# Joining pairs of states on VectorE before the accumulating transfer, in a Mamba and mixture-of-experts block

## The reference

```python
h = layernorm(x) * (1 + ca) + sa
x = x + ga * attn(h)                      # a Mamba layer
h = layernorm(x) * (1 + cb) + sb
x = x + gb * ffn(h)                       # a mixture of experts

# attn: 512 inner channels, 16 states
xi, z = split(rmsnorm(h) @ in_proj.T)
xi = silu(causal_conv4(xi))
dt, Bm, Cm = split(xi @ x_proj.T)         # 16, 16, 16
delta = softplus(dt @ dt_proj.T + b)
for every token:                          # per channel d and state s
    s = s * exp(delta * A) + delta * Bm * u
    y = sum_s(s * Cm)
y = (y + u * D) * silu(z);  out = y @ out_proj.T + h

# ffn: 16 experts, 4 of them per token, and a shared one of 256
g = sigmoid(h @ gate_w.T);  top4 of g, normalized -> combine
routed = sum_e combine_e * (silu(h @ win_e) * (h @ vin_e)) @ wout_e
```

## Time and profile before

| | |
|---|---|
| time, median of 3 runs | 2876.76 us (2871.17 to 2878.23) |
| the profiled execution | 2876.35 us, its span 2874.6 us |
| busy over the span | PE 2407.7 us, POOL 2400.2, DVE 2274.8, ACT 2127.2 |
| instructions | 52662 |
| mean granted TensorE clock | 0.943 of full speed |
| DMA | 456.03 MB, 159 GB/s |

### The profile page before, as it was taken

One profiled execution on the slowest core, in us unless ns is written; L12 is line 12 of the kernel. 1 busy time (PEld: TensorE's weight loads), 2 busy tenths in 40 slices (PEclk: granted clock), 3 DMA queues, 4 the chain that ended last, 5 costly groups with the idle time before them and its releaser, 6 DMA issues.

```text
span 2874.6 us, 52662 instructions
## 1 busy us (share of the span) xinstructions
PE 2407.7 (84%) x16372; PEld 1915.6 (67%) x16372; DVE 2274.8 (79%) x3495; ACT 2127.2 (74%) x4033; POOL 2400.2 (83%) x2382
## 2 busy tenths in 40 slices
PE   4557989879798897979889798988979888797989
PEld 1335767768576775857667576766857677585868
DVE  5777878788787878778787887878878787887853
ACT  4787877778687777877778787777868777786641
POOL 1887998889888898988989899898979988897942
PEclk7668999999999999999999999999999999999999
DMA  2786767867676785777768676786767777676841
GB/s 74 197 178 141 172 154 170 185 140 171 147 171 160 174 184 132 173 169 161 165 150 189 145 172 158 168 185 136 180 147 170 162 171 180 137 171 154 192 101 60
DMA packets 154565, 456.03 MB, mean 159 GB/s; under 512 B 22280, under 2 KB 24968, under 8 KB 154032
## 3 DMA queue, kind: packets, MB, share of 16 engines
q0 software_dynamic: 73728, 268.47, 49.1%
q1 hardware_dynamic: 80560, 184.20, 20.5%
HBM read 166.29 MB, written 17.87 MB: 64 GB/s over the span
## 4 chain that ended last, share of the span: by engine, by line
POOL 49%; issue 29%; DMA 10%; PE 2%; ACT 2%; DVE 2%; POOLq 1%; DVEq 0%; ACTq 0%; SPq 0%
POOL db_sb L701 26%; DMA y_sb<-c_rows 9%; POOL y_sb L713 9%; POOL act L744 7%; POOL y_sb L722 2%; POOL du_sb L688 2%; DMA w_sb<-w_dram 1%; POOL conv L679 1%; PE bank_ps L1461 1%; DVE states L1186 1%; POOLq L698 1%; PE moe_ps L1479 1%; POOL rstd L729 1%; PE bank_ps L1414 0%; ACT da_ps L945 0%
## 5 line engine op out<-in xcount | busy, mean ns | idle before, releaser
L701 POOL TENSOR_TENSOR db_sb<-du_sb,b_sb 128x512 f32<-128x512 f32 x1024 | 1653.2, 1991 | 103.8 <-DVE states L1186 103.2
L713 POOL DMA_DIRECT2D y_sb<-c_rows x512 | 745.1, 1455 | 159.7 <-DMA y_sb<-c_rows 92.9
L918 ACT ACTIVATE c_rows<-rows_ps,xd_sb 128x512 f32<-128x512 f32 x1024 | 687.0, 684 | 169.3 <-DMA y_sb<-c_rows 100.6
L744 POOL TENSOR_TENSOR act<-act,w_sb 128x256 f32<-128x256 f32 x512 | 689.3, 1515 | 119.6 <-DVE act L1273 97.2
L945 ACT ACTIVATE da_ps<-delta,a_sb 128x512 f32<-128x512 f32 x1024 | 702.9, 690 | 64.4 <-DVE states L1186 60.4
L1387 PE MATMUL rows_ps<-ident,states 128*128 128x128 f32 x4096 | 614.5, 287 | 145.2 <-DVE states L1186 91.4
L1461 PE MATMUL bank_ps<-h2T_high,ein_w_high 128*128 128x256 f16 x2304 | 638.2, 277 | 57.9 <-DVE act L1273 31.1
L1186 DVE TENSOR_TENSOR_SCAN states<-da_ps,carry,db_sb 128x512 f32<-128x512 f32 x512 | 643.9, 1274 | 26.1 <-ACT da_ps L945 18.5
L1479 PE MATMUL moe_ps<-eout_sb,act 128*128 128x256 f32 x2304 | 589.8, 388 | 75.0 <-POOL act L744 52.9
L1387 PEld LDWEIGHTS rows_ps<-ident,states 128*128 128x128 f32 x4096 | 502.1, 148 | 225.2 <-DVE states L1186 97.8
L1186 DVE TENSOR_TENSOR_SCAN states<-da_ps,db_sb 128x512 f32<-128x512 f32 x512 | 612.4, 1213 | 41.1 <-ACT da_ps L945 33.4
(11 more groups left out here) (170 smaller groups left out, 2678.5 us busy)
## 6 DMA issues: line engine op xcount, KB each, us to landing
y_sb<-c_rows POOLq DMA_DIRECT2D x512, 512.0 KB, 6.3
b_sb<-b_dram SPq DMA_DIRECT2D x128, 512.0 KB, 5.5
w_sb<-w_dram SPq DMA_DIRECT2D x256, 256.0 KB, 4.0
th_p<-x_dram SPq DMA_DIRECT2D x16, 512.0 KB, 6.9
r_dram<-conv SPq DMA_DIRECT2D x16, 512.0 KB, 2.9
x<-r_dram SPq DMA_DIRECT2D x16, 512.0 KB, 4.6
out_dram<-x SPq DMA_DIRECT2D x32, 256.0 KB, 4.7
mod_p<-mod_dram SPq DMA_DIRECT2D x7, 384.0 KB, 8.9
```

Of the source, the lines that this page charges most:

```text
L701: pool.tensor_tensor(db_sb[:, n % NDB, :], du_sb[:, slots[t][0][0], b, :], b_sb[:, k % NBPAIR, s % BPAIR, :], ALU.mult).then_inc(sem["scal ...
L713: pool.dma_start(y_sb[:, slots[t][0][0], CPAIR * pair:CPAIR * pair + CPAIR, :], c_rows[:, n % NCR, :, :], accum_op=ALU.add).then_inc(c_add ...
L744: pool.tensor_tensor(place, place, w_sb[:, k % NWROWS, n % WROWS, :], ALU.mult).then_inc(sem["e_weighed"], 1)
L918: ac.activation(c_rows[:, n % NCR, j % CPAIR, :], rows_ps[j % 2][:, :], ACT.Copy, scale=xd_sb[:, slots[t][0][0], j, s:s + 1]).then_inc(sem ...
```

## The change

Four things are changed.

1. For the states in `JOINED` (1, 5, 9, 13) the scaling by C_s is done on DVE instead of ACT, by an instruction that also adds the scaled rows of the state before, which lie in `c_rows`. The state before issues no transfer of its own; the transfer behind the joined state carries both.

```diff
+JOINED = (1, 5, 9, 13)
...
-            out.append((at + 0.145, ("c_scale", t, s, j)))
-            if j % CPAIR == CPAIR - 1:
+            out.append((at + 0.145, ("c_join" if s in JOINED else "c_scale", t, s, j)))
+            if j % CPAIR == CPAIR - 1 and s + 1 not in JOINED:
                 out.append((at + 0.892, ("c_add", t, s, j // CPAIR)))
...
             def c_scales(step, j):
-                return sem["c_scaled"], NJ * step + j + 1
+                k, s = divmod(step, NS)
+                joins = len(JOINED) * k + sum(q < s for q in JOINED)
+                if s in JOINED:
+                    return sem["c_joined"], NJ * joins + j + 1
+                return sem["c_scaled"], NJ * (step - joins) + j + 1
+
+            def piece(step, j):
+
+                k, s = divmod(step, NS)
+                return NJ // CPAIR * (step - len(JOINED) * k - sum(q <= s for q in JOINED)) + j // CPAIR
...
+                    def c_join(t, s, j):
+
+                        step = NS * nS(t) + s
+                        place = c_rows[:, piece(step, j) % NCR, j % CPAIR, :]
+                        v.wait_ge(sem["rows_full"], NJ * step + j + 1)
+                        v.wait_ge(*c_scales(step - 1, j))
+                        v.scalar_tensor_tensor(place, rows_ps[j % 2][:, :], xd_sb[:, slots[t][0][0], j, s:s + 1], place,
+                                               ALU.mult, ALU.add).then_inc(sem["c_joined"], 1)
```

```diff
-                        ac.activation(g_sb[:, :, :], bank(key)[:, 0:NJ * NE].rearrange("p (j e) -> p j e", j=NJ), ACT.Exp, scale=-1.0 / LIFT).then_inc(bank_read(key)[0], 1)
+                        ac.activation(bank(key)[:, 0:NJ * NE], bank(key)[:, 0:NJ * NE], ACT.Exp, scale=-1.0 / LIFT).then_inc(sem["logit_exped"], 1)
...
+                        exped, g, equal, rank = (bank(key)[:, n * NJ * NE:(n + 1) * NJ * NE] for n in range(4))
...
-                        done(v.tensor_scalar(g_sb[:, :, :], g_sb[:, :, :], 1.0, None, ALU.add))
-                        done(v.reciprocal(g[:, :, :], g_sb[:, :, :]))
+                        done(v.tensor_scalar(raised[:, :, :], grid[0], 1.0, None, ALU.add))
+                        done(v.reciprocal(grid[1], raised[:, :, :]))
...
-                        done(v.tensor_tensor(above[:, :, :], g[:, :, :], fourth, ALU.is_gt))
-                        done(v.tensor_tensor(equal[:, :, :], g[:, :, :], fourth, ALU.is_equal))
+                        done(v.tensor_tensor(above[:, :, :], grid[1], fourth, ALU.is_gt))
+                        done(v.tensor_tensor(grid[2], grid[1], fourth, ALU.is_equal))
```

4. All numbers of `SHIFT`, `PLACE`, `FIRST`, `LAST`, `START` and the scalars above them are new (120 lines), among them:

```diff
-TICK, ROUTED, UNITS_END = 1.4598, 16.0092, 63.8809
-SLOT = 70.5981
+TICK, ROUTED, UNITS_END = 1.4006, 15.946, 63.7625
+SLOT = 70.0828
```

More of the change, by code:

```diff
@@ L137, in mix_steps @@
     return out
-LEAD_P0, LEAD_P, LEAD_M = 16.5692, 7.9826, 18.1414
-TICK, ROUTED, UNITS_END = 1.4598, 16.0092, 63.8809
-SOFT = 45.3931
-Z_AHEAD, Y_SOON, Y_LATE = 0.8485, -5.3218, 0.8267
-SLOT = 70.5981
[L145 to L159, removed]
@@ L248 @@
-START = {"a_made": 0.992, "constants": -1.608, "ct_silu": -9.647, "ct_tanh": -6.912, "first_loads": 4.989, "fold": 3.908,
-         "in_high": -10.598, "in_low": 4.148, "mod0": -2.429, "mod0_gate": 0.385, "mod0_rows": 0.709, "mod_rows": -3.599,
-         "mod_store": -7.158, "mods": -4.917, "norm_lift": 9.587, "out_scale": 0.531}
+LEAD_P0, LEAD_P, LEAD_M = 9.4848, 7.9681, 36.993
+TICK, ROUTED, UNITS_END = 1.4006, 15.946, 63.7625
+SOFT = 45.4792
+Z_AHEAD, Y_SOON, Y_LATE = -0.3185, 22.219, -0.2513
@@ new lines @@
+SLOT = 70.0828
+SHIFT = {"a_made": -20.502, "b_load": -2.232, "b_store": -0.217, "c_add": 1.069, "c_join": 0.148, "c_scale": 0.685, "carry": 0.601,
+         "constants": 10.315, "ct_silu": 2.578, "ct_tanh": 8.345, "delta": -0.261, "dt_bias": -0.862, "dt_high": -1.482, "dt_low": -0.332,
+         "dtp": 0.392, "du": -1.586, "e_act": -0.172, "e_mul": -0.078, "e_tanh": -0.47, "e_weigh": 0.942, "ein_high": -7.634,
+         "ein_load": 3.221, "ein_low": -3.584, "eout_fold": -5.781, "eout_load": 29.252, "exp": 1.008, "expert_in": -0.139,
+         "expert_out": 0.842, "first_loads": -2.625, "fold": -2.807, "gather": 0.59, "h2_high": 1.243, "h2_low": 0.757, "h2_scale": 0.021,
+         "h2_t": 1.411, "h_rms": -1.74, "h_scale": -0.139, "h_square": 0.621, "hn_high": 0.107, "hn_low": 0.848, "hn_t": -1.363,
+         "in_high": -2.02, "in_low": -7.498, "logit": -0.08, "logit_exp": 1.812, "mod0": -12.588, "mod0_gate": 19.972, "mod0_rows": -1.064,
+         "mod_m_load": 8.559, "mod_p_load": -6.842, "mod_rows": 29.353, "mod_store": -4.702, "mods": -2.473, "norm_lift": -7.161,
+         "op": 1.418, "op_gate": 1.599, "out_add": 0.9, "out_gate": 0.183, "out_scale": 8.16, "out_store": 1.711, "r_add": 6.003,
+         "r_gate": 0.061, "r_load": 7.615, "r_store": -1.548, "router": 1.815, "rows": 0.254, "scaled": 0.757, "scan": -0.083,
+         "skip": -1.043, "skip_evac": 0.781, "skip_t": -0.141, "soft_exp": -1.963, "soft_ln": 0.343, "tap": 0.071, "u": -0.57,
+         "u_tanh": -0.321, "w_evac": -0.184, "w_load": -0.355, "w_store": -3.245, "w_t": 0.292, "x1": 1.086, "x1_norm": -0.819,
+         "x1_rstd": -2.814, "x1_stat": 1.324, "x_load": -1.588, "x_norm": 1.465, "x_rstd": 1.249, "x_scale": 0.453, "x_shift": -0.228,
+         "x_stat": 0.847, "xd": -0.781, "xd_evac": 0.619, "xd_t": -0.431, "xd_t_evac": -1.669, "xi": -0.046, "xi_center": 0.137,
+         "xi_copy": 0.05, "y_evac": 0.895, "y_gate": 0.739, "y_t": 0.967, "z": -1.779, "z_gate": -0.572, "z_tanh": -0.612}
@@ new lines @@
+PLACE = {"b_load_0": -4.611, "b_load_1": 10.996, "b_load_2": 6.227, "b_load_3": -3.389, "b_load_4": 4.088, "b_load_5": 5.136,
[49 rows of a table added]
+         "hn_t_1": -3.219, "in_high": -8.239, "in_low": 5.818, "logit": 1.913, "logit_exp": -0.292, "mod_m_load": -1.37,
+         "mod_p_load": 1.265, "op_0": 1.103, "op_1": 0.564, "op_2": 0.206, "op_3": -2.3, "op_gate_0": -0.794, "op_gate_1": -0.426,
+         "op_gate_2": 0.141, "op_gate_3": -13.342, "out_add_0": 0.478, "out_add_1": 3.252, "out_gate_0": 0.038, "out_gate_1": -0.223,
+         "out_store_0": 5.292, "out_store_1": 2.506, "r_add": 0.146, "r_gate": -0.302, "r_load": -0.81, "r_store": 8.339, "router": 0.163,
[21 rows of a table added]
@@ new lines @@
+LAST = {"e_act": -0.013, "e_mul": 0.055, "e_tanh": 7.665, "e_weigh": 9.991, "expert_in": 1.282, "expert_out": 1.728, "h2_high": -2.579,
+        "h2_low": -1.883, "h2_scale": -3.705, "h2_t": -3.18, "logit": -5.063, "logit_exp": -1.443, "op": -1.223, "op_gate": 0.698,
+        "out_add": 0.395, "out_gate": 1.049, "out_store": 2.058, "r_load": 1.578, "router": -1.085, "w_evac": 7.703, "w_load": 4.992,
+        "w_store": 0.751, "w_t": 1.21, "x1": 0.98, "x1_norm": -2.829, "x1_rstd": -3.726, "x1_stat": 0.952, "y_evac": 0.855,
+        "y_gate": -1.648, "y_t": -1.423, "z": -3.218, "z_gate": -0.524, "z_tanh": -0.384}
@@ L253, in place @@
+START = {"a_made": -11.043, "constants": 1.985, "ct_silu": -17.265, "ct_tanh": -17.277, "first_loads": 14.92, "fold": 1.506,
+         "in_high": 5.735, "in_low": 6.141, "mod0": 1.888, "mod0_gate": 2.156, "mod0_rows": -12.33, "mod_rows": -0.854,
+         "mod_store": 16.464, "mods": -15.099, "norm_lift": 17.774, "out_scale": 3.712}
 def place(what):
-    return "_".join(str(n) for n in (what[0], *(what[3:] if what[0] in ("exp", "scaled", "scan", "rows", "c_scale", "c_add") else what[2:])))
+    return "_".join(str(n) for n in (what[0], *(what[3:] if what[0] in ("exp", "scaled", "scan", "rows", "c_scale", "c_join", "c_add") else what[2:])))
@@ L394, in adaln_block @@
         wT = sb("wT", [NE, CH])[:, :]
-        g_sb = sb("g_sb", [P, NJ, NE])
-        rt = [sb(f"rt{n}", [P, NJ, NE]) for n in range(4)]
+        raised, above, below = (sb(name, [P, NJ, NE]) for name in ("raised", "above", "below"))
         rt_small = [sb(f"rt_small{n}", [P, NJ]) for n in range(2)]
@@ L705, in c_add @@
                         step = NS * nS(t) + s
-                        n = NJ // CPAIR * step + pair
+                        n = piece(step, CPAIR * pair)
                         pool.wait_ge(*c_scales(step, CPAIR * pair + CPAIR - 1))
@@ L913, in c_scale @@
                         step = NS * nS(t) + s
-                        n = NJ // CPAIR * step + j // CPAIR
+                        n = piece(step, j)
                         ac.wait_ge(sem["rows_full"], NJ * step + j + 1)
@@ L1228, in done @@
                             v.wait_ge(sem["router_step"], own[0])
-                        v.wait_ge(sem["const_made"], 6)
-                        above, equal, rank, g = rt[0], rt[1], rt[2], rt[3]
+                        key = ("logit", t)
+                        exped, g, equal, rank = (bank(key)[:, n * NJ * NE:(n + 1) * NJ * NE] for n in range(4))
+                        grid = [place.rearrange("p (j e) -> p j e", j=NJ) for place in (exped, g, equal, rank)]
                         count, total = rt_small
-                        v.wait_ge(*bank_read(("logit", t)))
```

(28 more changed lines are left out.)

47 lines of the change are left out of this document (14 added, 33 removed), and 140 rows, old and new, of the table PLACE.

## The result

The changed kernel takes 2784.18 us (median of 4 runs, 2781.71 to 2787.70), the kernel before 2877.49 us. The ratio is 0.9679, 95% interval 0.9665 to 0.9693: 93 us less, where 56 were forecast. The profiled execution of the changed kernel has a span of 2779.9 us.

The account below looks back on a forecast made before the run. POOL was taken as the main chain, with 49% of the span. The terms summed to -4.6 us a slot, -3.5 after a quarter off for PE, so -56 us over 16 slots: 2820 us, range 2772 to 2880.

Parts of the forecast that it names:

- A: The forecast itself: 2820 us, own range 2795 to 2848, chance 0.50.
- Part 1: 384 accumulating transfers in place of 512 spare POOL 6.6 us a slot, of which 5.0 count as gain.
- C: Rival: the transfers were hidden, so POOL's idle time rises by what its busy time falls; 2860 us, chance 0.20.
- Part 2: POOL's waits for earlier accumulating transfers: 1.0 us a slot gained, between a loss of 2 and a gain of 5.6.
- The holding of the ring: Two of the three row buffers are held from one state into the next: at worst part 2 loses 2 us.
- Part 3: Sixteen `c_join` a slot on DVE replace ACT scalings: 1.5 and 1.0 us a slot lost, bounds 0 to 10.6.
- D: Rival: joins on DVE wait 0.8 us each for PE's rows; 2929 us, chance 0.19 with D2 and a worse order.
- D2: Rival: joins on DVE are held up like L1234, 1.9 us each; some 3010 us, chance included in D's 0.19.
- Part 4: The router on DVE, with its source in PSUM, gets 2.1 us a slot shorter, bounds 0 and 3.4.
- Part 5: The logits' bank, one of three, comes free some 5 us later: 0.5 us a slot lost, between 0 and 2.
- Part 6: Dropping 18 hidden `keep_awake` matmuls a slot on PE may lower its clock: 0.5 us lost, bounds -1 and 3.
- Part 7: New constants ordering the queues: taken as 0, bounded at 2 us a slot either way.

Follow-up runs that it names:

- only scaled: The changed kernel with states 1, 5, 9, 13 scaled on DVE but not joined, all 512 transfers still issued: 2827.6 us, ratio 0.9840 to the kernel before.

## Why the prediction was right, and where it was not

The direction and the chain were right: POOL was short, the joins relieve it, and the time is in the range of 2772 to 2880, though faster than the 2795 to 2848 that A gave itself. The sum of 93 us came about otherwise than by the forecast's terms. The parts that the forecast priced, with the old places, gave 27 us, half of its 56; the places, priced at nothing, gave the rest. That the total lies in the range is in good part luck.

- **Part 1, the transfers' issue.** POOL's busy time fell by 7.5 us a slot, 6.6 forecast, and the slot by 6.4. POOL's idle time grew by only 1.1 (21.5 for 20.4), so the sign of C didn't appear. Right.
- **Part 2, waits on transfers.** Taken as 1.0 us a slot. The waits went from 92.9 to 2.0 us on POOL and from 100.6 to 3.8 on ACT. A part of that is the new order's, since without joins it had 31.8 and 26.7. The holding of the ring, feared as a loss of 2, shows in no wait for a transfer. But POOL's waits for rows took their place, so its idle time in front of the transfers is what it was. Parts 1 and 2 together, as measured by joined against only scaled, gave 46 us, 2.9 a slot, where 6.0 less a quarter was counted.
- **Part 3, the joins on DVE.** Each took 738 ns by its record for the 751 of the row it was priced by, and their wait was 2.1 us in all; rivals D and D2 are out. But the term's sign was wrong where it was measured by itself, in the new order: not 2.5 us a slot lost, but 15 us in all gained. ACT "is the least loaded; I give that nothing" was the mistake: ACT had time, but others waited for its queue, PE for the row buffers (115.3 us, then 69.3) and DVE for tanh and exponential. The joins alone, all three parts, were forecast at 42 us and gave 49 in the old order, 61 in the new. The 49 include a router that was 2.1 us shorter, which no part of the sum had as an effect of the joins.
- **Part 4, the router.** 2.17 us shorter, 2.1 forecast, and the reason given stands. What it is worth, with part 5, hangs on the rest: nothing alone, a loss of 30 us beside the joins in the old order, 27 us gained in the new. The sum added parts 1 and 4 as if they were apart, but the wait hangs on POOL's products being under way when the router starts, and the joins can change that. The reading of the stages was loose too: of the router from 947.90 to 953.58 only the last 2.6 us lie in the stage of 951 to 965 that was called the router's.
- **Part 5, the bank held.** Priced at 0.5 us a slot; a term of the wrong size: alone in the old order it took all of part 4's 2.1, and with joins it cost 30 us. PE's wait moved from the weights to `xi`. In the new order `xi` of the second channel block stands ahead of the router and of the second expert unit, so the walk gives it the bank of the first expert unit, not the one of the logits. Its wait of 46.1 us is for that unit's `e_mul`. With the router in SBUF the walk gives it the logits' bank, free after the exponential, and no such wait is recorded.
- **Part 6, `keep_awake`.** 8 us forecast as a loss; nothing in the old order, 12 us in the new. The steady part's clock fell from 0.97 to 0.94 in the change, and is 0.97 again with the matmuls back: the clock was the part that showed, not the matmuls' own time.
- **Part 7, the places.** This step failed. Taken as 0 and bounded at 2 us a slot, they cost 19 us alone and give 65 us (4 a slot) with the other three parts in. The bound from a tenth of POOL's idle time had no ground. An order is made for certain durations and held buffers, and here both had changed; in particular the old one makes `xi` wait for the router's bank, and the new one doesn't. PE's wait at the weights, whose growth I had named as a sign against, is 2.2 us.

Open: what in the new order costs 19 us when nothing else is changed (the grown waits for ACT's scalings are a sign, not a proof), and how the 65 us divide among its moves. The places were tried as one block.

## What to carry to other kernels

Where both the issue of accumulating transfers and the wait for earlier ones stand in the chain, as here, summing pairs before the transfer relieves both. The engine with the most idle time can still be the one that others wait for: moving work from it to a busier one gained 15 us here. A resource held longer (here one of three banks) can eat a whole gain on the path; it shows as a wait in front of the next step that needs it. Two parts of a change can take away the same wait, as the joins and the router's move did, so don't add their gains before looking. Price a new order only together with the change it belongs to: alone it lost, and without it less than a third of the gain remained.

## What the runs showed of the hardware that I had not expected

The wait of a small DVE instruction beside a busy POOL isn't tied to one instruction. Take away the `tensor_scalar` that waits 1.9 us, and the next one with two inputs in SBUF waits 1.26 (1486 ns for 225). It goes with POOL's work: with the joins alone, where the router is in SBUF but no product of POOL was under way at its start, the same `tensor_scalar` took 162 to 195 ns sixteen times. In PSUM, with one SBUF input at most in each step, the router took 4.42 to 4.44 us in each of the 16 slots that have one.

With eighteen matmuls a slot whose results nobody reads, the mean granted clock was 0.939 and not 0.921, PE's other matmuls were 3.4 us a slot shorter, and the time 12 us less. In the old order (0.943 and not 0.936) they did nothing for the time.
